# A decoder layer on one core: GpSimd's residual adds behind the smoothing, one batch's statistics moved, quantisation's small operands to GpSimd

## What is computed

```
x = x + attention(layernorm(x))
x = x + smooth_quant_mlp(layernorm(x), fside, ctx)
x = x + routed_ffn(layernorm(x))
```

```
ch_bias = (max(xp, rows) + min(xp, rows)) / 2
xz = xp - ch_bias
scale = tmax / 2 ** (7 - idx) / 7
y = result @ w_dq.T + ch_bias @ w_orig.T + b
```

## Time and profile before

| | |
|---|---|
| median of 3 runs | 944.46 us (943.44 to 945.13) |
| profiled execution | 946.15 us, its span 944.3 us |
| mean granted TensorE clock | 0.888 of full speed |
| busy, share of the span | TensorE 78%, VectorE 79%, ScalarE 63%, GpSimd 18% |
| chain that ended last | TensorE 23%, VectorE 17%, ScalarE 4%, issue 2%, transfers 2%, GpSimd 1% |
| first quantisation and projections | about 58 to 150 us |
| attention | 150 to 480 us |
| second quantisation, output projection | 483 to 531 us |
| second layer | 531 to 720 us |
| a VectorE product group / a reduction in a wide step | 2.72 us for four / 2.28 us |
| routing and feed-forward | 720 to 944 us |

### The profile page before, as it was taken

The page is one execution under the profiler, slowest core; times in us unless marked ns, Lnnn a source line. Parts: engine busy times, 40 slices in busy tenths (PEclk is TensorE's granted clock), DMA queues, the critical chain, the costliest instruction groups (busy, mean ns, idle before and its releaser), DMA issues. The chain is left out here.

```text
span 944.3 us, 15550 instructions
## 1 busy us (share of the span) xinstructions
PE 735.3 (78%) x5125; PEld 312.4 (33%) x5141; DVE 746.8 (79%) x1047; ACT 594.6 (63%) x1051; POOL 171.3 (18%) x263
## 2 busy tenths in 40 slices
PE   1567998999999999999946525654558279999997
PEld 0532332222222222222221124443436134444443
DVE  7999788999999999999999888798989764621111
ACT  4868645988988889889949036655447719651000
POOL 1200753011111221111220500122003130000010
PEclk9978997999999999999976857767777669999999
DMA  8600774122222222222140001200109520000000
GB/s 311 222 1 1 230 248 138 52 62 66 72 61 64 82 61 63 73 59 64 36 157 0 1 0 44 68 23 0 13 0 355 191 78 1 1 1 11 23 23 34
DMA packets 51597, 70.62 MB, mean 75 GB/s; under 512 B 13108, under 2 KB 27476, under 8 KB 51040
## 3 DMA queue, kind: packets, MB, share of 16 engines
q1 hardware_dynamic: 50272, 65.84, 22.0%
q0 software_dynamic: 1280, 4.20, 1.4%
HBM read 46.17 MB, written 19.12 MB: 69 GB/s over the span
## 5 line engine op out<-in xcount | busy, mean ns | idle before, releaser
L982 DVE TENSOR_REDUCE SWV<-PS 128x2 f32<-128x1024 f32 x256 | 300.7, 1214 | 16.0 <-PE PS L1437 14.9
L1871 ACT ACTIVATE slab<-PS 128x512 f32<-128x512 f32 x512 | 275.6, 595 | 36.0 <-PE PS L1570 28.1
L1553 PE MATMUL PS<-slab,HB 128*32 128x256 f32 x2048 | 164.5, 394 | 10.4 <-ACT HB L1855 10.4
L1570 PE MATMUL PS<-slab 50*128 50x512 f16 x512 | 124.9, 385 | 2.8 <-ACT slab L1871 0.3
L1437 PE MATMUL PS<-slab 48*128 48x512 f16 x512 | 101.1, 392 | 2.3 <-ACT slab L1827 1.3
L1744 PE MATMUL PS<-slab 128*128 128x512 f16 x384 | 86.3, 388 | 1.7 <-DVE slab L1326 1.4
L1755 PE MATMUL PS<-slab 128*128 128x512 f16 x384 | 83.0, 379 | 0.0
L1553 PEld LDWEIGHTS PS<-slab,HB 128*32 128x32 f32 x2048 | 41.8, 108 | 91.1 <-issue 64.6
L1358 DVE SCALAR_TENSOR_TENSOR WOT<-PS,cmax,WOT 128x512 f32<-128x512 f32 x8 | 6.0, 751 | 69.8 <-PE PS L1755 69.8
L1437 PEld LDWEIGHTS PS<-slab 48*128 48x128 f16 x512 | 24.6, 93 | 103.3 <-issue 94.9
L1352 DVE SCALAR_TENSOR_TENSOR slab<-HB,cmax,slab 128x512 f16<-128x512 f32 x32 | 23.8, 750 | 43.6 <-ACT slab L1964 43.6
(11 more groups left out here) (309 smaller groups left out, 1180.2 us busy)
## 6 DMA issues: line engine op xcount, KB each, us to landing
slab<-in_L_ffn_w SPq DMA_DIRECT2D x2, 4096.0 KB, 14.6
q_split<-slab SPq DMA_DIRECT2D x24, 256.0 KB, 2.7
k_split<-slab SPq DMA_DIRECT2D x24, 256.0 KB, 2.7
slab<-q_split SPq DMA_DIRECT2D x64, 96.0 KB, 2.6
slab<-k_split SPq DMA_DIRECT2D x64, 96.0 KB, 2.6
slab<-in_x SPq DMA_DIRECT2D x4, 1024.0 KB, 12.1
slab<-HB SPq DMA_DIRECT2D x128, 32.0 KB
slab<-in_fside_BxS2xS SPq DMA_DIRECT2D x4, 1024.0 KB, 5.5
```

What stands on the lines that cost most here:

```text
L982: nc.vector.tensor_reduce(NM[:, ring].rearrange("p (a x) -> p a x", a=2)[:, :, x], PS[:, bank:bank + 2, :], AX.X, ALU.max, negate=True).th ...
L1553: ins = nc.tensor.matmul(PS[32 * h:32 * h + 32, 6, cols], VST[:, r % 2, k, h, :], PROB[:, k, h, cols], start=k == half == 0, stop=k == KB ...
L1570: nc.tensor.matmul(PS[:, st_bank(2 * s + a), :], KP[rows, r, p, P * k:P * k + P], QP[rows, r, p, :], start=True, stop=True).then_inc(st_re ...
L1871: nc.scalar.activation(PROB[:, k, 2 * a + p], PS[:, st_bank(t), :], ACT.Exp, scale=score_scale).then_inc(probs, 1)
```

## The change

GpSimd's `added(n)` waits in addition for `l_xs` to reach 2n + 5, the end of the smoothing of x in step n + 2. The statistics of batch 1 are written ahead of `prepare(0)`. In both quantisations the repeated biases, the picks and s0col, and in the first the scales AQ, are made by GpSimd behind its all-reduce; the factor `DH ** -0.5` moves into `qk_scale`, which takes one more small VectorE operation. `identh` is cast at the start. Semaphore counts follow.

```diff
@@ gpsimd, quantise(k), behind partition_all_reduce
+                pool.wait_ge(cbt_scaled, k)
+                nc.gpsimd.tensor_copy(CBX[k - 1].rearrange("p c (b g n) -> p (c b) g n", b=B, g=4),
+                                      small["mn"][:, :].rearrange("p (c n) -> p c n", n=NC // B).unsqueeze(2).broadcast_to(
+                                          [P, CT * B, 4, NC // B])).then_inc(cbt_ready, 1)
+                for n, m in enumerate(((0, 1, 2), (3,))[k - 1]):
+                    ins = nc.gpsimd.tensor_tensor(PICKS[k - 1][n].rearrange("p (b g n) -> p b g n", b=B, g=4),
+                                                  s0i[0:4, :].rearrange("p (b n) -> p b n", b=B).unsqueeze(2).broadcast_to(
+                                                      [4, B, 4, NC // B]),
+                                                  identf[0:4, m:m + 1].unsqueeze(1).unsqueeze(3).broadcast_to(
+                                                      [4, B, 4, NC // B]), ALU.mult)
+                ins.then_inc(cbt_ready, 1)
+                pool.wait_ge(cbt_ready, 2 * k)
+                for u in range(2):
+                    ins = nc.gpsimd.tensor_copy(s0col[64 * u:64 * u + 64, :],
+                                                s0[64 * u:64 * u + 64, :].rearrange("p (t u) -> p u t", u=2)[:, u])
+                if k == 1:
+                    own(ins)
+                    projection_scales()
+                else:
+                    ins.then_inc(ab_ready, 1)
...
@@ gpsimd, added(n)
                 pool.wait_ge(l_h, 4 * n + 4)
+                pool.wait_ge(l_xs, 2 * n + 5)
@@ vector, start
+            own(nc.vector.tensor_copy(identh, identf[:, :]))
@@ vector, scales_of_scores
-                own(nc.vector.tensor_scalar(qk_scale[:, 0:2], bounds[:, 2:4], QK_TOP, None, ALU.mult))
+                own(nc.vector.tensor_scalar(qk_scale[:, 0:1], bounds[:, 2:3], QK_TOP, DH ** -0.5, ALU.mult, ALU.mult))
+                own(nc.vector.tensor_scalar(qk_scale[:, 1:2], bounds[:, 3:4], QK_TOP, None, ALU.mult))
@@ vector, quantise(k)
-                own(nc.vector.tensor_tensor(flat["mn"]...
+                nc.vector.tensor_tensor(flat["mn"]...
+                                            [P, CT, B, NC // B]), ALU.mult).then_inc(cbt_scaled, 1)
-                nc.vector.tensor_copy(CBX[k - 1]...
-                for n, m in enumerate(((0, 1, 2), (3,))[k - 1]):
-                    ins = nc.vector.tensor_scalar(PICKS[k - 1][n]...
-                ins.then_inc(cbt_ready, 1)
...
-                for u in range(2):
-                    ins = nc.vector.tensor_copy(s0col[64 * u:64 * u + 64, :]...
-                    own(ins)
                 bias_parts()
-                if k == 1:
-                    projection_scales()
+                dve.wait_ge(ab_ready, k)
...
-            nc.vector.tensor_copy(identh, identf[:, :]).then_inc(identh_ready, 1)
@@ vector, ahead of the second layer's loop
             second_norm(0)
-            prepare(0)
             other_half_done(KB)
             statistics(KB, 2 * KB)
+            prepare(0)
             second_norm(1)
@@ tensor, chunk_bias
-                pe.wait_ge(cbt_ready, k)
+                pe.wait_ge(cbt_ready, 2 * k)
@@ scalar, value_copy(u)
+                if u == 0:
+                    act.wait_ge(ab_ready, 1)
```

More of the change, by code:

```diff
@@ L334, in decoder_kernel @@
         qk_mm, qk_scaled, qk_h, qk_l = (sem(n) for n in ("qk_mm", "qk_scaled", "qk_h", "qk_l"))
-        bound_ready, bounds_ready, scale_ready, kp_ready, identh_ready = (
-            sem(n) for n in ("bound_ready", "bounds_ready", "scale_ready", "kp_ready", "identh_ready"))
+        bound_ready, bounds_ready, scale_ready, kp_ready, cbt_scaled = (
+            sem(n) for n in ("bound_ready", "bounds_ready", "scale_ready", "kp_ready", "cbt_scaled"))
         split_out = [sem(f"split_out{r}") for r in range(3)]
@@ L614, in quantise, with projection_scales @@
                 nc.gpsimd.partition_all_reduce(tmaxb[:, :], tm[:, :], P, RMAX).then_inc(tmax_ready, 1)
+                pool.wait_ge(cbt_scaled, k)
[18 more added lines that the diff above has]
+                    ins.then_inc(ab_ready, 1)
+            def projection_scales():
+                for m in range(2):
+                    ins = nc.gpsimd.tensor_tensor(AQ[:, m], s0[:, :].unsqueeze(1).broadcast_to([P, CT, NC]),
+                                                  sw[:, m].unsqueeze(2).broadcast_to([P, CT, NC]), ALU.mult)
+                own(ins)
+                for m in range(2):
+                    ins = nc.gpsimd.tensor_tensor(AQ[:, m], AQ[:, m], qk_scale[:, m:m + 1].unsqueeze(2).broadcast_to([P, CT, NC]),
+                                                  ALU.mult)
+                ins.then_inc(ab_ready, 1)
             pool.wait_ge(consts, 3)
@@ L841, in chunk_bias_parts @@
                 ins.then_inc(cbp_ready, 1)
[L843 to L847, removed]
-                own(ins)
-                nc.vector.tensor_scalar(AQ[:, 0], AQ[:, 0], qk_scale[:, 0:1], DH ** -0.5, ALU.mult, ALU.mult).then_inc(ab_ready, 1)
-                nc.vector.tensor_scalar(AQ[:, 1], AQ[:, 1], qk_scale[:, 1:2], None, ALU.mult).then_inc(ab_ready, 1)
-                dve.wait_ge(ab_ready, 2)
             def scaled(u):
@@ L896, in quantise @@
                 own(nc.vector.reciprocal(s0i[:, :], s0[:, :]))
[L897 to L902, removed]
-                for n, m in enumerate(((0, 1, 2), (3,))[k - 1]):
-                    ins = nc.vector.tensor_scalar(PICKS[k - 1][n].rearrange("p (b g n) -> p b g n", b=B, g=4),
-                                                  s0i[0:4, :].rearrange("p (b n) -> p b n", b=B).unsqueeze(2).broadcast_to(
-                                                      [4, B, 4, NC // B]), identf[0:4, m:m + 1], None, ALU.mult)
-                ins.then_inc(cbt_ready, 1)
+                nc.vector.tensor_tensor(flat["mn"].rearrange("p (c b n) -> p c b n", b=B, c=CT), over_channels(s["cbias"]),
+                                        s0i[:, :].rearrange("p (b n) -> p b n", b=B).unsqueeze(1).broadcast_to(
+                                            [P, CT, B, NC // B]), ALU.mult).then_inc(cbt_scaled, 1)
                 own(nc.vector.tensor_scalar(tm[:, :].bitcast(U32), tmaxb[:, :].bitcast(U32), 23, None, ALU.logical_shift_right))
@@ L936, in quantise @@
                     one_pass(kind, 0, Q_HALF)
-                for u in range(2):
-                    ins = nc.vector.tensor_copy(s0col[64 * u:64 * u + 64, :],
-                                                s0[64 * u:64 * u + 64, :].rearrange("p (t u) -> p u t", u=2)[:, u])
-                    own(ins)
                 bias_parts()
-                if k == 1:
-                    projection_scales()
+                dve.wait_ge(ab_ready, k)
                 for u, kind in enumerate(PASSES):
@@ L1374, in _ @@
             pe.wait_ge(consts, 4)
-            pe.wait_ge(dve_own, 3)
+            pe.wait_ge(dve_own, 4)
             nc.tensor.matmul(PS[:, 7, :].rearrange("p (j c) -> p j c", c=CHUNK),
@@ L1515, in _ @@
                 if u == TURN_AT:
-                    pe.wait_ge(identh_ready, 1)
                     pe.wait_ge(v_scaled, u)
```

## The result

The changed kernel takes 953.45 us (median of 4 runs, 952.59 to 954.65), the kernel before 943.95 us beside it (943.00 to 945.13). The ratio is 1.0099, with a 95% interval of 1.0085 to 1.0112: 9.3 us slower (8.0 to 10.6). The medians themselves differ by 9.5. The forecast was 952.9, in a range of 943.5 to 957.0.

The account below looks back on a forecast made before the run. The chain was taken to pass through VectorE in both quantisations and the second layer, and TensorE in projections and feed-forward. Terms -8.6 - 1.6 + 15.7 + 2.9 = +8.4 on 944.46 gave 952.9 us, range 943.5 to 957.0.

Parts of the forecast that it names:

- C: First quantisation: picks moved to GpSimd come late, so TensorE's bias products and VectorE's bias parts start late; +15.7 us.
- the swap: Both quantisations: GpSimd idles to change code before the picks' tensor_tensor, behind the all-reduce and copy; taken as 6.95 us.
- the turns: Quantisations: GpSimd and VectorE exclude each other for whole instructions, so each pick waits out one long VectorE operation (subtraction 4.42 us).
- D: Second quantisation: the one pick waits for the end of rounding, and VectorE's bias parts start later; +2.9 us.
- rival 4: Second quantisation: GpSimd's code change takes over 8.1 us, so the pick waits for scaling too; 957.4 us, chance 0.05.
- B: Start of the second layer: statistics ahead of the maxima fill VectorE's idle time, smoothing starts earlier; -1.6 us.
- A: Second layer, steps 4 and 5: GpSimd's adds wait for the smoothing, so both `both_roots` stalls go; -8.6 us.
- What is late next: Second layer, step 5: TensorE's products of step 4 want ScalarE's last copy, said to stay covered by 1.2 us.
- A swap that costs nothing: Both quantisations: the code change on GpSimd ahead of the picks costs no time; 933.0 us, chance 0.09.
- Three picks together: First quantisation: all three picks pass after one wait for VectorE's subtraction; 944.2 us, chance 0.09.
- Adds that block the smoothing: Second layer: GpSimd's delayed add blocks the smoothing of w instead, so nothing is gained there; 961.5 us, chance 0.03.
- A longer swap: Same as rival 4: over 8.1 us in the second quantisation, the pick waits for scaling too; 957.4 us, chance 0.05.

## Why the prediction was right, and where a size was off

**C, the first quantisation (+15.7; the attention ends 15.6 later).** The mechanism held link by link up to the bias parts: the idle time put down to issue 6.95 (taken: 6.95), the last pick at 80.7 (81.0), TensorE's products from 80.85 to 97.06 or 16.2 us (16.8), VectorE's bias parts at 97.16 (97.95). The copy of 512 elements took 0.61 (0.6). The step that looked weakest, that three picks of a few hundred elements would cost three VectorE operations of 4.4 us, is what two runs show from both sides: the one with one instruction instead of three (the attention then ends at 487.24, 4.7 after the kernel before, with 0.9 us won already at the all-reduce), and the one with a fourth operation in the queue. The run with the picks on VectorE shows that the swap and the turns cost time only where someone waits for them. How much of the loss the swap alone has was not measured: no run keeps the picks on GpSimd without it.

That the sum of C came out within 0.1 is in part luck, three sizes that cancel. The bias parts shifted by 16.2 instead of 17.0. From them to the third projection the forecast took 10.14 us, and it was 11.36 (97.16 to 108.52), because TensorE was at a low clock there, which the prediction's sum had at nothing:

```profile
106.17 1.89 PE L1494 MATMUL PS<-WB,slab 128*128 128x512 bf16 x4
```

In the kernel before the same four took 1.04 (at 89.77). The granted clock between 105 and 109 us is 0.58 here, and 0.96 between 88 and 92 us there. From there to the end of the attention 1.33 us were won back (16.89 to 15.56), where 0.81 was forecast for `identh`. That term was mis-sized: it was read from one wait, and the runs above give the edit 1.7 to 2.4.

**D, the second (+2.9; +2.8).** From +15.56 to +18.37. The pick waited for one operation, the end of rounding, as said; the swap of 6.77 stayed under the 8.1 us of rival 4.

**B, the statistics (-1.6; -1.6).** +18.37 to +16.75, and 1.7 by the run that has it alone.

**A, the adds (-8.6; -7.55).** The operations of 4.45 and 4.47 take 0.17, and the shift falls from 16.73 at step 3 (614.52 to 631.25) to 7.75 at step 5, by 8.98: the 8.6, and 0.4 because TensorE spread the roots of step 4 faster (16 matmuls in 2.05 us instead of 3.78). Then step 6 gives 1.46 back, by its products (5.31 against 3.40 us) and the two waits of VectorE behind them. "What is late next" was looked for in ScalarE's copies of step 4 with 1.2 us of slack. That slack was not there: it rested on a spreading of about 4 us in step 5, which took 2.05, and TensorE waited 0.69 for the copies, without VectorE waiting behind. What cost time was the clock, one step on, and the prediction had no term for it.

Why the clock was lower in the products of step 6 stays open. TensorE had idled 7.99 us ahead of the spread of step 5's scales, where before it had idled 6.09, which looks like a reason. But in the run with the earlier swap it idled the same 7.99, and the products ran at 1.00 and took 3.63. Over the kernels without the stalls, the trace gives A as 7.5 to 8.8 us between the smoothings of step 3 and step 7, and the run that has it alone gives 6.5 (5.0 to 7.9) by the ratio.

**The sum.** 15.56 + 2.81 - 1.62 - 7.55 = +9.2, measured +9.5 in the medians, forecast +8.4. Against the forecast, A is 1.05 higher, and the other three together are 0.25 lower.

**The rivals.** A swap that costs nothing (933.0): it is there, 6.77 to 7.46 us, in the quantisations of every kernel that has a tensor_tensor behind the all-reduce there, and TensorE waited behind it. Three picks together (944.2): they took turns. Adds that block the smoothing (961.5): the smoothing took 4.48 beside the add, with `both_roots` at 0.17. A longer swap (957.4): 6.77 in the second quantisation, under the 8.1 that it needed.

## What to carry to other kernels

Before a small operation is moved to GpSimd, look at who waits for it and at what VectorE does in that moment: the price is not its own 0.2 to 0.6 us. It is the rest of the long two-input VectorE instruction under way, once for each instruction in the queue, and some 7 us besides where, as here, a tensor_tensor follows an all-reduce. If it has to be there, one instruction with many elements was far cheaper than several with few (9 us here), and work that nobody waits for goes behind it. The same edits with the picks left on VectorE are 1.5% faster than the kernel before instead of 1% slower. And a wait that one profile shows can be less than what its removal brings, if an operation ahead of it ran at a lower clock in that execution (0.81 us shown, 1.7 to 2.4 won).

## What the runs showed of the hardware that was not expected

- Between two long VectorE instructions a pick costs VectorE only 0.08 us (4.50 instead of 4.42), not the 0.26 to 0.39 us that it takes by itself. A pick of 384 elements in one instruction cost 0.51 (4.93).
- Which GpSimd operations are separated by the idle time: none stands between the all-reduce and a copy but the wait for the input, none between a tensor_tensor and a copy; a tensor_tensor behind the all-reduce and copies has 6.77 to 7.46 us, in all six kernels that have the pair in the quantisations. Behind the all-reduce of `bounds`, at 37 us, all eleven kernels have it (6.93 to 7.78), and one element is enough for it (7.04 and 6.81).
- Two edits that were expected to gain 1.6 and 0.8 us gained 3.0 and 2.8 by the ratio (3.1 and 2.2 by the medians). For the second, the traces show 2.4 at the end of the attention. For the first, 1.4 us stay unexplained: its trace shows 1.7 to 1.9 up to the end of the loop. Executions do differ by as much where no edit touches them: step 2 of the second layer, for one, takes 18.8 us in three of the profiled executions and 20.2 to 20.5 in the others, the kernel before among them. Whether that is the reason was not shown.
